# A selective-scan stage in which VectorE empties the front's PSUM bank and GpSimd multiplies by the C rows in single 512-column operations

## The reference, cut to what matters

```python
xc   = silu(causal_conv4(x_in, conv_w, conv_b))          # 512 channels, 2048 tokens, 2 sequences
proj = xc @ xp_w.T                                       # 64 columns for dt, 16 for B, 16 for C
dt   = softplus(dt_part @ dt_w.T + dt_b)
h    = exp(dt[:, :, None] * A) * h + (dt * x)[:, :, None] * B[:, None, :]   # 16 states per channel
y    = einsum('bdn,bn->bd', h, C) + D * x
```

## Time and profile before

| what | value |
|---|---|
| median of 3 runs | 4641.67 us (4637.85 to 4651.1) |
| the profiled execution | 4628.16 us |
| its span | 4626.6 us |
| scan stage, first to last scan | 251.8 to 2046.9 us |
| busy over the span: TensorE / VectorE / ScalarE / GpSimd | 77 / 61 / 59 / 38 % |

### The profile page before, as it was taken

One profiled execution on the slowest core, in us unless ns is written; L12 is line 12 of the kernel. 1 busy time (PEld: TensorE's weight loads), 2 busy tenths in 40 slices (PEclk: granted clock), 3 DMA queues, 4 the chain that ended last, 5 costly groups with the idle time before them and its releaser, 6 DMA issues. The chain is left out here.

```text
span 4626.6 us, 69508 instructions
## 1 busy us (share of the span) xinstructions
PE 3557.3 (77%) x20742; PEld 2201.9 (48%) x20742; DVE 2819.4 (61%) x4258; ACT 2720.9 (59%) x4311; POOL 1749.6 (38%) x1132
## 2 busy tenths in 40 slices
PE   8477777777777777756775888888988885499990
PEld 4156666666666666645553222222222223366660
DVE  4267777777777777756675666666666665411105
ACT  3288888888888888864563455555555551011120
POOL 0067777777777777764342000000000002300006
PEclk9688889998888888877886899999999997699995
DMA  6443322233333333334545000100010103311115
GB/s 209 120 110 83 83 83 83 83 96 87 88 88 84 83 86 89 83 105 147 208 155 163 17 24 24 26 24 20 24 26 24 26 17 117 122 64 67 69 40 185
DMA packets 183442, 385.72 MB, mean 83 GB/s; under 512 B 21763, under 2 KB 96630, under 8 KB 168624
## 3 DMA queue, kind: packets, MB, share of 16 engines
q1 hardware_dynamic: 129360, 285.61, 21.3%
q10 hardware_dynamic: 39760, 51.81, 3.3%
q0 software_dynamic: 13968, 43.97, 2.8%
HBM read 272.97 MB, written 110.91 MB: 83 GB/s over the span
## 5 line engine op out<-in xcount | busy, mean ns | idle before, releaser
L730 DVE TENSOR_TENSOR_SCAN scan_hh<-scan_dA,scan_state,scan_bx 128x512 f32<-128x512 f32 x1024 | 1247.9, 1265 | 413.6 <-PE scan_bx L816 351.6
L507 POOL TENSOR_TENSOR scan_hC<-scan_hh,scan_cbc 128x1024 f32<-128x1024 f32 x512 | 1207.7, 2370 | 237.4 <-DVE scan_hh L730 137.2
L1464 DVE TENSOR_REDUCE attend_mx<-attend_s 128x1 f32<-128x512 f32 (+1 forms) x1360 | 781.5, 608 | 342.9 <-PE attend_s L1594 226.0
L816 PE MATMUL scan_bx<-kept_ident,scan_dBxT 128*128 128x128 f32 x4096 | 692.8, 297 | 104.6 <-DVE scan_hh L730 55.1
L573 ACT ACTIVATE scan_dBxT<-scan_dtxT,scan_bt 128x512 f32<-128x512 f32 x1028 | 655.8, 712 | 97.8 <-PE scan_bx L816 97.7
L826 PE MATMUL scan_acc<-kept_ident,scan_hC 128*128 128x128 f32 x4128 | 671.8, 292 | 43.1 <-ACT scan_uu L582 41.8
L568 ACT ACTIVATE scan_dA<-scan_dt,scan_an 128x512 f32<-128x512 f32 x1028 | 665.7, 714 | 50.6 <-DVE scan_hh L730 50.6
L816 PEld LDWEIGHTS scan_bx<-kept_ident,scan_dBxT 128*128 128x128 f32 x4096 | 525.5, 154 | 297.4 <-DVE scan_hh L730 154.2
L1558 ACT ACTIVATE attend_full<-attend_s 128x1024 f32<-128x1024 f32 x384 | 392.0, 1025 | 332.1 <-PE attend_s L1621 328.1
L1594 PE MATMUL attend_s<-attend_kt,attend_qt 96*128 96x512 bf16 (+1 forms) x1360 | 481.4, 372 | 130.9 <-DVE attend_mx L1464 73.3
L826 PEld LDWEIGHTS scan_acc<-kept_ident,scan_hC 128*128 128x128 f32 x4128 | 538.8, 153 | 47.2 <-ACT scan_uu L582 45.5
(11 more groups left out here) (219 smaller groups left out, 4502.3 us busy)
## 6 DMA issues: line engine op xcount, KB each, us to landing
scan_xs<-scratch_xin SPq DMA_DIRECT2D x288, 256.0 KB, 7.7
scan_cbc<-scratch_crows SPq DMA_DIRECT2D x64, 1024.0 KB, 5.0
scratch_qk<-mix_heads ACTq DMA_DIRECT2D x64, 384.0 KB, 10.0
scratch_y<-scan_uu ACTq DMA_DIRECT2D x17, 1024.0 KB, 4.2
attend_qt<-scratch_qk SPq DMA_DIRECT2D x34, 384.0 KB, 3.7
attend_kt<-scratch_qk SPq DMA_DIRECT2D x34, 384.0 KB, 4.5
mix_yf<-scratch_y SPq DMA_DIRECT2D x10, 1024.0 KB, 8.3
mix_yb<-scratch_y SPq DMA_DIRECT2D x10, 1024.0 KB, 12.0
```

Source lines behind the costliest of these rows:

```text
L507: pool.tensor_tensor(hC[n % 2][:, ms, :], h[:, ms, :], rows.unsqueeze(1).broadcast_to([P, 2, C]), ALU.mult).then_inc(hc_ok, 1)
L730: dve.tensor_tensor_scan(hh[n % 2][:, m, r], dA[n % 2][:, m, r], bx[bank(j)][:, r], state[:, d, n, m:m + 1], ALU.mult, ALU.add).then_inc(h ...
L816: last = pe.transpose(bx[bank(j)][:, t * P:(t + 1) * P], dBxT[turned_slot(n)][:, t, m * P:(m + 1) * P], k["ident"][:, :])
L1464: dve.tensor_reduce(mx[:, t, c:c + 1], s1[v % 2][:, 0:w], AX_X, ALU.max).then_inc(s1_read, 1)
```

## The change

Four things are altered together, all in the scan stage. VectorE, not ScalarE, empties the front's bank after convolutions and turnings. The four convolutions stand together (sub-steps 29, 33, 38, 43), ahead of the turnings, and AT_LAST is gone. SyncE issues the inputs of convolution piece 2 behind C-row group 2 and those of piece 3 ahead of C-row group 3. ScalarE's silu moves from tail(0), where it served the next unit, to tail(12), where it serves the unit two ahead; before the first unit it therefore runs once more. GpSimd multiplies in four operations of 512 columns per n, and the waits on its semaphore `hc_ok` count four per n; the save of the state stands before the fourth.

```diff
--- before.py
+++ after.py
@@ -386,12 +386,12 @@
         xinv = xin.rearrange("b (m g r) l -> b m r g l", g=COLS, r=STRIP)
         block = s.block()
 
-        FR_PROJ, FR_BT, FR_DT, FR_NEXT, FR_TURN, FR_LAST, FR_ALL = 0, 1, 2, 6, 9, 13, 14
+        FR_PROJ, FR_BT, FR_DT, FR_NEXT, FR_TURN, FR_ALL = 0, 1, 2, 6, 10, 14
         FR_BEGIN = 18
 
         HELD_HC, HELD_H, HELD_SAVED, HELD_BX = 16, 8, 2, 8
         LAG = 8
-        AT_DT, AT_NEXT, AT_TURN, AT_LAST, AT_SKIP = (18, 21, 24, 27), (30, 36, 41), (49, 51, 53, 55), 58, (14, 16, 19, 22)
+        AT_DT, AT_NEXT, AT_TURN, AT_SKIP = (18, 21, 24, 27), (29, 33, 38, 43), (49, 51, 53, 55), (14, 16, 19, 22)
 
         def bank(j):
             return 1 if j == SUB - 1 else j % 3
@@ -435,7 +435,7 @@
                 sp.dma_start(crows[d], pr[RANK:RANK + NS, :]).then_inc(stored_c, 16)
 
             def load_c(f, d, g):
-                sp.wait_ge(hc_ok, (f * NS + g * GROUP - 2 * GROUP) * 2 + 2 * GROUP + HELD_HC)
+                sp.wait_ge(hc_ok, (f * NS + g * GROUP - GROUP) * DT + HELD_HC)
                 sp.dma_start(cbc[g % 2][:, :, :],
                              crows[d:d + 1, g * GROUP:(g + 1) * GROUP, :].broadcast_to([P, GROUP, C])
                              ).then_inc(loaded_c[g % 2], 16)
@@ -465,12 +465,12 @@
                         hold(sp, k)
                         for m in range(2):
                             load_x(nb, nc_, d, m)
-                        for g in range(2, 4):
-                            load_c(f, d, g)
+                        load_c(f, d, 2)
                         for m in range(2, DT):
                             sp.wait_ge(fr_mm, first + FR_NEXT + m - 1)
                             hold(sp, k)
                             load_x(nb, nc_, d, m)
+                        load_c(f, d, 3)
 
         @block.gpsimd
         def _(pool):
@@ -497,29 +497,19 @@
                             edge = C - 1 if d == 0 else 0
                             if n % GROUP == 0:
                                 pool.wait_ge(loaded_c[n // GROUP % 2], f * 32 + (n // GROUP // 2) * 16 + 16)
-                            for half in range(2):
-                                ms = slice(2 * half, 2 * half + 2)
-                                pool.wait_ge(h_ok, q * DT + 2 * half + 2 + HELD_H)
-                                if half:
+                            for m in range(DT):
+                                pool.wait_ge(h_ok, q * DT + m + 1 + HELD_H)
+                                if m == DT - 1:
                                     hold(pool, k)
                                     pool.tensor_copy(state[:, d, n, :], h[:, :, edge]).then_inc(saved, 1)
-                                pool.wait_ge(acc_ok, q * DT + 2 * half + 2)
-                                pool.tensor_tensor(hC[n % 2][:, ms, :], h[:, ms, :],
-                                                   rows.unsqueeze(1).broadcast_to([P, 2, C]), ALU.mult
+                                pool.wait_ge(acc_ok, q * DT + m + 1)
+                                pool.tensor_tensor(hC[n % 2][:, m, :], h[:, m, :], rows, ALU.mult
                                                    ).then_inc(hc_ok, 1)
                             if n == 6:
                                 front_relu_and_e(1 - d, f + 1)
 
         @block.scalar
         def _(act):
-            def conv_out(d, f, m, group):
-                if m == 0 and not (isinstance(f, int) and f < 2):
-
-                    act.wait_ge(skip_ok, f - 1)
-                    act.wait_ge(front_ok, f - 1)
-                act.wait_ge(fr_mm, group + 1)
-                act.activation(xc[d][:, m, :], fr[:, :], ACT.Identity, bias=cb[:, d, m:m + 1]).then_inc(fr_out, 1)
-
             def silu(d, f, group):
 
                 act.wait_ge(fr_out, group + 1)
@@ -544,10 +534,6 @@
                     act.wait_ge(dt_ok, f)
                 act.wait_ge(relu_ok, f * DT + m + 1)
                 act.activation(ee[:, m, :], fr[:, :], ACT.Abs, bias=db[:, d, m:m + 1]).then_inc(fr_out, 1)
-
-            def turned_out(d, j, group):
-                act.wait_ge(fr_mm, group + 1)
-                act.activation(dtxT[d][:, j, :], fr[:, :], ACT.Copy).then_inc(fr_out, 1)
 
             def front_exp(f, group):
 
@@ -587,8 +573,6 @@
 
             act.wait_ge(a_raw, 1)
             act.activation(an[:, :, :, :], an[:, :, :, :], ACT.Exp).then_inc(a_raw, 1)
-            for m in range(DT):
-                conv_out(0, 0, m, m)
             silu(0, 0, 3)
             proj_out(0, 4)
             bt_out(0, 5)
@@ -597,10 +581,7 @@
             front_exp(0, 9)
             front_one_plus(0)
             front_log(0)
-            for j in range(JT):
-                turned_out(0, j, 10 + j)
-            for m in range(DT):
-                conv_out(1, 1, m, 14 + m)
+            silu(1, 1, 17)
             act.wait_ge(a_ready, 1)
             act.wait_ge(dt_ok, 1)
             for m in range(DT):
@@ -627,26 +608,16 @@
                         front_one_plus(g)
                     if n == 9:
                         front_log(g)
-                    if n == 11:
-                        conv_out(d, f + 2, 2, first + FR_NEXT + 2)
-                    if n in (13, 14):
-                        turned_out(o, 2 * n - 25, first + FR_TURN + 2 * n - 25)
-                    if n == 15:
-                        conv_out(d, f + 2, 3, first + FR_LAST)
 
                 def tail(n):
-                    if n == 0:
-                        silu(o, g, first - 1)
                     if n == 3:
                         store(f)
                     if n == 4:
                         dt_out(o, g, 0, first + FR_DT)
                     if n == 6:
                         dt_out(o, g, 3, first + FR_DT + 3)
-                    if n in (8, 9):
-                        conv_out(d, f + 2, n - 8, first + FR_NEXT + n - 8)
-                    if n in (12, 13):
-                        turned_out(o, 2 * n - 24, first + FR_TURN + 2 * n - 24)
+                    if n == 12:
+                        silu(d, f + 2, first + FR_NEXT + 3)
 
                 for n in range(NS):
                     q = f * NS + n
@@ -705,6 +676,13 @@
                 dve.wait_ge(dt_ok, f + 1)
                 dve.tensor_tensor(dtx[:, :, :], dt[d][:, :, :], xc[d][:, :, :], ALU.mult).then_inc(front_ok, 1)
 
+            def conv_out(d, f, m, group):
+                if m == 0 and not (isinstance(f, int) and f < 2):
+                    dve.wait_ge(skip_ok, f - 1)
+                    dve.wait_ge(front_ok, f - 1)
+                dve.wait_ge(fr_mm, group + 1)
+                dve.tensor_scalar(xc[d][:, m, :], fr[:, :], cb[:, d, m:m + 1], None, ALU.add).then_inc(fr_out, 1)
+
             def relu(d, f, m, group):
                 if m == 0 and not (isinstance(f, int) and f == 0):
                     dve.wait_ge(dt_ok, f)
@@ -712,11 +690,22 @@
                 dve.tensor_scalar(dt[d][:, m, :], fr[:, :], db[:, d, m:m + 1], 0.0, ALU.add, ALU.max
                                   ).then_inc(relu_ok, 1)
 
+            def turned_out(d, j, group):
+                dve.wait_ge(fr_mm, group + 1)
+                dve.tensor_copy(dtxT[d][:, j, :], fr[:, :]).then_inc(fr_out, 1)
+
+            for m in range(DT):
+                conv_out(0, 0, m, m)
             for m in range(DT):
                 relu(0, 0, m, 6 + m)
             softplus_low(0, 0)
             softplus(0, 0)
             times_x(0, 0)
+            for j in range(JT):
+                turned_out(0, j, 10 + j)
+            for m in range(DT):
+                conv_out(1, 1, m, 14 + m)
+
             def scan(d, f, n, m):
                 j = n * DT + m
                 q = f * NS + n
@@ -724,8 +713,7 @@
                 dve.wait_ge(da_ok, f * SUB + j + 1)
                 if m == 0:
                     dve.wait_ge(saved, q + 1)
-                if m % 2 == 0:
-                    dve.wait_ge(hc_ok, q * 2 + m // 2 + HELD_HC - 3)
+                dve.wait_ge(hc_ok, (q - 2) * DT + m + 1 + HELD_HC)
                 r = slice(None) if d == 0 else slice(None, None, -1)
                 dve.tensor_tensor_scan(hh[n % 2][:, m, r], dA[n % 2][:, m, r], bx[bank(j)][:, r],
                                        state[:, d, n, m:m + 1], ALU.mult, ALU.add).then_inc(h_ok, 1)
@@ -741,6 +729,12 @@
                         if at in AT_DT:
                             i = AT_DT.index(at)
                             relu(o, g, i, first + FR_DT + i)
+                        if at in AT_NEXT:
+                            i = AT_NEXT.index(at)
+                            conv_out(d, f + 2, i, first + FR_NEXT + i)
+                        if at in AT_TURN:
+                            i = AT_TURN.index(at)
+                            turned_out(o, i, first + FR_TURN + i)
                     if n == 8:
                         softplus_low(o, g)
                     if n == 9:
@@ -819,7 +813,7 @@
 
             def add(f, a):
                 n, m = a // DT, a % DT
```

(4 more changed lines are left out.)

## The result

The changed kernel takes 4526.44 us (median of 4 runs, 4520.1 to 4530.42) where the kernel before takes 4646.39 (4 runs, 4637.85 to 4652.92). The ratio is 0.9742, with a 95% interval from 0.972 to 0.9764. The forecast was 4502 us, 139.5 us less than before; measured are 120 us less.

The account below looks back on a forecast made before the run. Bound: a chain of waits passing from engine to engine. Stretches of 16.9 + 26.9 + 31.6 + 28.9 = 104.3 us save 9.0 a unit, 144 over sixteen, less 4.5 for the extra silu: 4641.7 - 139.5 = 4502 us, range 4455 to 4590.

Parts of the forecast that it names:

- the signs that I had called wrong: VectorE or TensorE waiting for hC; late ScalarE decays at n=14; L507 over 1.4 us; TensorE awaiting piece 2 inputs or emptyings.
- First stretch: Sub-steps 0 to 12: 21.99 us to 16.9, saved 5.1, bounds 0 and 7.4, as silu and one emptying leave ScalarE.
- Second stretch: Sub-steps 12 to 28, 26.92 us: no change taken; bounds -1 and +1.
- Third stretch: Sub-steps 28 to 44: 36.73 us to 31.6, saved 5.1; bounds 7.8 saved and 2.6 lost.
- The wait that convolution 0 at 29 brings: Ahead of scan 29: convolution 0 must wait until ScalarE has emptied the last dt product; 1.3 us.
- The 0.6 for a convolution at the lower clock: Convolution 3 at sub-step 43, soon after a TensorE pause, would take 1.93 instead of 1.06 us; 0.6 added.
- the 0.8 for GpSimd's work without a gap: Sub-steps 28 to 44: GpSimd has gapless work when VectorE's three two-input operations come; 0.8 us wait added.
- rival D: Piece 2 input late, SyncE waiting at C-row group 2 or transfers sharing bandwidth; 3.6 a unit back, 4560 us; chance 0.04.
- Last stretch: Sub-steps 44 to 64 and the edge: 27.62 us to 28.9, 1.25 lost; bounds 0 lost and 6 lost.
- rival C: silu at n = 12 not covered: 4.5 us a unit comes back, 4574 us; chance 0.08.
- a pitch of 1.19 us per product: GpSimd's 512-column products in the scan stage: 1.19 us each, bounds 1.155 and 1.28, taken as no change.
- Rival E: GpSimd becomes the bound from sub-step 28 on; at 1.6 us per product 115.7 us a unit, 4700 us; chance 0.08.

Follow-up runs that it names:

- The early save: Changed kernel with GpSimd's save of the state ahead of all four products, for n = 7 alone: 4524.55 us, ratio 0.9738.
- the halves: Changed kernel with GpSimd multiplying again in two operations of 1024 columns per n: 4534.81 us, ratio 0.9758.

## Why the prediction was right, and what was mis-sized

**The chain moved as described.** The unit was priced as waits passed from engine to engine. Traced unit against traced unit it lost 7.13 us, 113.26 to 106.13, where 9.0 was forecast. The mean unit lost 6.8. None of the rivals came true. Of the signs that I had called wrong three are there, all small. VectorE waits 0.43 us for hC ahead of scan 21. TensorE waits for hC at L820, 25.2 us in 38 places over the stage. And it waits 0.73 us for each of the first three emptyings between 49 and 58, behind which VectorE's scans run on without a gap.

**First stretch.** 16.9 forecast, 17.22 measured, saved 4.8 instead of 5.1. The evacuation starts 13.5 us behind the edge (687.68), forecast 13.2. Undoing silu's move alone costs 4.8 us a unit and brings TensorE's wait for silu back, which shows the cause.

**Second stretch.** No change was forecast, +0.17 was measured.

**Third stretch, the step with the largest error.** 31.6 forecast, 32.46 measured. The wait that convolution 0 at 29 brings was forecast at 1.3 and is 1.37. The 0.6 for a convolution at the lower clock was not paid: all four took 1.06 or 1.07 us, and the granted clock is 0.95 there instead of 0.81. That this 0.6 was not due hid part of the error, which is luck. The mis-sized term is the 0.8 for GpSimd's work without a gap. It comes to 1.39 ahead of scan 36, where I had looked at hC only and not at the save, which the change puts behind three products, one of them stretched by VectorE's own operation, plus 0.82 by which L677 (3.09) is longer than the 2.27 I had used. The early save and the halves each removed the first; the halves made the second larger. That the input of piece 2 would arrive in time held, and the transfers' order is worth 11.5 us a unit inside the changed kernel and 2.8 in the one before. I had credited it with 3.64 and had not seen that the other parts depend on it: rival D has the late input at 4560 us, and the run with it took 4718.23.

**Last stretch.** 28.9 forecast, 29.36 measured. silu at step 12 is covered: ScalarE starts it at 756.51, and its next decays are done at 766.05, 2.25 us ahead of scan 56; a cover of 2 us or more was forecast. That rules out rival C. The stretch grew by 1.7 us instead of 1.3.

**GpSimd.** I took a pitch of 1.19 us per product, bounds 1.155 and 1.28. The instructions of L506 (min/median/max):

```profile
L506 POOL TENSOR_TENSOR scan_hC<-scan_hh,scan_cbc x1024: 1255/1280/3455, 255.9 to 1943.0; 128x512 f32<-128x512 f32 x171
```

Four in a row take 4.99, a pitch of 1.24; the median is the upper bound, 1.28. The row of another stage that gave 1.155 was not the like: its second input, mix_parts, is bfloat16. The long ones stand where VectorE's two-input operations run: four products take 7.05 us from 739.22, beside L672, where 4.99 is usual. Rival E, GpSimd as the bound, needed 1.55 and did not come near; in the traced unit GpSimd is busy 92.8 of 106.1 us.

**The sum.** By the profiled executions 139.5 - 100.8 = 38.7 us are missing. Of these 35.1 are in the stage (144 forecast, 108.9 measured), of which 1.83 x 16 = 29 are the four stretches' errors. Most of the rest comes from pricing one unit 16 times: the traced unit lost 7.13 us and the mean one 6.8, which is 5 us over 16. The first scan came 2.6 later, not 4.5, which gives 1.9 back, and 5.5 are behind the scan. By the medians 120 us went where 139.5 were forecast, and the median of before has itself moved from 4641.7 to 4646.4 with a fourth run; so the forecast of 4502 is 24 us low.

That 2.6 is near 4.5 is luck. The first scan starts at 251.8 in the kernel before, at 254.4 in the changed one, at 245.8 with silu's move undone and at 259.7 with the emptyings on ScalarE again. So the additional silu costs 8.6 or 7.9 us there, and the emptyings on VectorE, which I put at nothing ahead of the first unit, give back 6.0 or 5.3. Single profiles of kernels with the same start differ by up to 3 us (251.8 to 254.9 for that of the kernel before), so each of these differences is good to about that.

**What stays open.** Why the silu before the first unit costs some 8 us, more than its own 4.5, was not looked into. Of how the parts depend on each other, only the transfers and the products were measured from both sides; silu and the emptyings were only undone, not tried alone, and the earlier places of the convolutions were not undone by themselves. The parts undone one by one cost 4.8, 3.4 and 11.5 us a unit, 19.7 together, where the whole change won 6.8. So they can't be added up as shares of the gain.

## What to carry to other kernels

When four engines are nearly equally busy, price a unit stretch by stretch from the one that all must pass, and ask of each wait which instruction ends it: here 7 of 113 us came from moving work, and none from less of it. A transfer's place in the issuing queue is part of any schedule: with the consumers moved earlier and the queue left as it was, the same change is 1.5% slower than no change. Splitting an operation to let consumers start sooner also moves what stands behind the pieces; here it delayed a small save and gained nothing by itself.

## What the runs showed of the hardware

- A VectorE operation of 2048 columns with two SBUF inputs takes 2.27 us when no GpSimd product holds it up (L666). Of the 16 of each line in the changed kernel, L672 takes 2.97 and L677 3.09 us on average beside products of 1.28 us; with products of 2.37 us L674 and L679 take 3.88 and 3.89. In the traced units the excess is about what is left of the product that runs when the operation comes: L677 starts at 747.93, 0.9 us ahead of that product's end, and is 0.82 longer. The other way round a GpSimd product is stretched, up to 3.46 us. This is what the Trainium skill (SBUF — State Buffer, Who interferes with whom) states of the two engines' shared port, and the trace agrees. The eight emptyings out of PSUM, 0.724 and 0.666 us on average, were not lengthened: the longest are 0.753 and 0.692.
- Two float32 products of 512 columns cost GpSimd 2.48 us in pitch where one of 1024 costs 2.33: 0.15 for the additional instruction.
- A releaser named by the profile was wrong at the edge and right at sub-step 36. At the edge the distance from the other candidate's start (1.43 and 1.44 us) and the count that the code waits for show it; at sub-step 36 an edit does.
